# A decoder's delta-rule stage: one convolution step, one gate and two weight splits stand earlier in the engines' orders

## The reference

```python
mixed_qkv = einsum('bsh,ch->bcs', hidden, Wqkv)          # q, k: 16 heads of 128; v: 32 heads of 128
z = einsum('bsh,vh->bsv', hidden, Wz)
b, a = hidden @ Wb.T, hidden @ Wa.T
mixed_qkv = silu(causal_depthwise_conv(mixed_qkv, conv_w))   # four taps along the tokens
beta = sigmoid(b);  g = -exp(A_log) * softplus(a + dt_bias)
# per head, token by token, q and k made unit vectors first, two value heads to a key head:
state = state * exp(g_t)
delta = (v_t - state^T k_t) * b_t
state = state + k_t (x) delta;  out_t = state^T q_t
core_n = out * rsqrt(mean(out^2) + eps) * norm_w * silu(z)
result = einsum('bsv,hv->bsh', core_n, Wout)
x = layernorm(x + result)
```

## Time and profile before

| | us |
|---|---|
| median of 3 executions (3673.87 to 3677.07) | 3675.44 |
| the profiled execution's own time | 3675.6 |
| its span | 3673.6 |
| busy in the span: PE, PEld | 3177.1, 2215.0 |
| busy in the span: DVE, ACT, POOL | 2612.0, 2096.6, 1442.7 |

### The profile page before, as it was taken

The page is one execution under the profiler, slowest core; times in us unless marked ns, Lnnn a source line. Parts: engine busy times, 40 slices in busy tenths (PEclk is TensorE's granted clock), DMA queues, the critical chain, the costliest instruction groups (busy, mean ns, idle before and its releaser), DMA issues. The chain is left out here.

```text
span 3673.6 us, 81792 instructions
## 1 busy us (share of the span) xinstructions
PE 3177.1 (86%) x29389; PEld 2215.0 (60%) x29408; DVE 2612.0 (71%) x4893; ACT 2096.6 (57%) x5396; POOL 1442.7 (39%) x1753
## 2 busy tenths in 40 slices
PE   7999688437999999999999999999999999984185
PEld 5777455225676666666666667666666666762042
DVE  2333499883777777777777777677777777776896
ACT  3333300134767776677766777677776777763453
POOL 1111154103545555455544545445454454530000
PEclk9999899767999999999999999999999999996598
DMA  2000111001010010110101000111001010101201
GB/s 109 12 13 7 77 39 36 26 20 44 13 42 31 25 31 20 42 30 25 31 23 38 30 25 31 26 36 31 24 31 34 28 35 20 31 19 46 92 1 46
DMA packets 43227, 120.67 MB, mean 33 GB/s; under 512 B 5824, under 2 KB 10048, under 8 KB 39488
## 3 DMA queue, kind: packets, MB, share of 16 engines
q1 hardware_dynamic: 42816, 115.30, 9.8%
HBM read 110.75 MB, written 4.54 MB: 31 GB/s over the span
## 5 line engine op out<-in xcount | busy, mean ns | idle before, releaser
L1856 DVE TENSOR_TENSOR delta_Pb<-delta_bank,delta_lev 128x512 f16<-128x512 f32 x448 | 311.1, 694 | 240.0 <-PE delta_bank L2182 240.0
L1848 DVE SCALAR_TENSOR_TENSOR delta_F<-delta_bank,delta_cw,delta_F 128x510 f32<-128x510 f32 (+1 forms) x512 | 381.1, 744 | 66.0 <-ACT delta_far L1667 56.0
L1434 POOL TENSOR_SCALAR_AFFINE_SELECT delta_LA<-delta_LA 128x512 f32<-128x512 f32 x128 | 81.2, 635 | 858.5 <-DVE delta_LA L1877 849.2
L2156 PE MATMUL delta_bank<-delta_xh,delta_qkvh 128*128 128x512 f16 x1024 | 392.3, 383 | 4.5 <-DVE delta_qkvl L1816 3.0
L2156 PE MATMUL delta_bank<-delta_xl,delta_qkvh 128*128 128x512 f16 x1024 | 391.8, 383 | 0.0
L2156 PE MATMUL delta_bank<-delta_xh,delta_qkvl 128*128 128x512 f16 x1024 | 390.7, 382 | 0.0
L1454 POOL TENSOR_TENSOR delta_F<-delta_F,delta_far 128x506 f32<-128x506 f32 x256 | 283.2, 1106 | 256.1 <-DVE delta_F L1848 256.1
L1865 DVE CAST delta_XT<-delta_bank 128x512 f16<-128x512 f32 x448 | 309.7, 691 | 45.4 <-PE delta_bank L2205 45.2
L1661 ACT ACTIVATE delta_F<-delta_bank,delta_cw 128x512 f32<-128x512 f32 x256 | 178.2, 696 | 279.9 <-PE delta_bank L2156 279.7
L1626 ACT ACTIVATE delta_Xi<-delta_bank 128x512 f16<-128x512 f32 x320 | 189.9, 593 | 186.7 <-PE delta_bank L2201 186.7
L2141 PE MATMUL delta_bank<-delta_zh,delta_xh 128*128 128x256 f16 x1024 | 279.7, 273 | 0.6 <-ACT delta_gz L1689 0.6
(11 more groups left out here) (313 smaller groups left out, 9268.5 us busy)
## 6 DMA issues: line engine op xcount, KB each, us to landing
delta_Gb<-g_rows SPq DMA_DIRECT2D x66, 512.0 KB, 5.3
delta_st_qkv<-in_Wqkv SPq DMA_DIRECT2D x17, 1024.0 KB, 8.1
conv_T<-filters SPq DMA_DIRECT2D x32, 256.0 KB, 3.1
delta_st_zo<-in_Wz SPq DMA_DIRECT2D x16, 512.0 KB, 8.4
delta_st_zo<-in_Wout SPq DMA_DIRECT2D x16, 512.0 KB, 6.2
ffn_ahead_W<-in_W SPq DMA_DIRECT2D x2, 4096.0 KB, 17.4
conv_ahead_C<-in_ctx_rev SPq DMA_DIRECT2D x1, 6144.0 KB, 17.7
attn_xt<-in_xT SPq DMA_DIRECT2D x8, 512.0 KB, 3.8
```

The costliest lines, as they stand in the source:

```text
L1848: ve.scalar_tensor_tensor(dst, src, cw_tap(i, 3 - lag), dst, ALU.mult, ALU.add)\
L1856: ve.tensor_tensor(left(Pb[:, lvl, :, :], lvl), comp(bank[5], lvl), bc(lev[:, lvl, :].rearrange("p (n s) -> p n s", s=1 << lvl), 1, 8), AL ...
L2156: ins = te.matmul(bk[:, :], ww[:, QKV[job], kc, :], xx[:, kc, tok:tok + 512], start=(m == 0), stop=(m == 11))
```

## The change

On ACT, the two `next_o` move from behind `gate(0)` to two earlier places: the first ahead of `silu_job("q")`, the second ahead of `output_high(0)`. `gate(1)` moves from behind `level_x(2, 1)` to ahead of `silu_job("v1")`. On DVE, `next_o(0)` moves to ahead of the lags of `v0`, `next_o(1)` to where `next_o(0)` stood, and the second lag of `v1` to ahead of `level_p(2, 1)`. The instructions themselves, their sizes and their waits stay as they are, and nothing moves on PE, POOL or SP.

```diff
@@ ACT, turn @@
                 token_major(0)
+                next_o(0)
                 silu_job("q")
                 conv_tap("v0")
                 token_major(1)
                 first_answer(0)
                 silu_job("k")
+                next_o(1)
                 output_high(0)
                 output_high(1)
                 silu_job("v0")
                 gate(0)
-                next_o(0)
-                next_o(1)
                 conv_tap("v1")
                 level_x(1, 1)
                 next_qkv(0)
                 next_qkv(1)
                 first_answer(1)
+                gate(1)
                 silu_job("v1")
                 next_qkv(2)
                 level_x(2, 1)
-                gate(1)
@@ DVE, turn @@
                 level_p(0, 1)
+                next_o(0)
                 conv_lag("v0", 1, 2)
...
                 query_norm()
-                next_o(0)
+                next_o(1)
                 second_chunk()
-                conv_lag("v1", 1)
+                conv_lag("v1", 1, 2)
                 level_p(2, 1)
-                conv_lag("v1", 2)
-                next_o(1)
                 level_xt(1, 1)
```

## The result

| | before | changed |
|---|---|---|
| median, us | 3674.99 (6 runs, 3671.79 to 3677.07) | 3647.34 (6 runs, 3646.79 to 3650.75) |
| ratio | | 0.9927, 95% interval 0.9914 to 0.9939 |
| span of the profiled execution | 3673.6 | 3645.0 |

The changed kernel is 27.65 us faster; 28.4 was forecast. That the sum is this close is partly luck, as the experiments show: one term was too small, another, taken as nothing, had a cost, and the units in which the loop branches back gained more than was reckoned.

A forecast was written before the change was run, and what follows sets the result against it. PE was taken to set the pace, busy 86% of the span. Gate 17.8 plus splits 10.6, with swap and moved splits' cost 0, made 28.4 us off 3675.4: 3647.0 us, range 3638 to 3661.

The forecast's parts named there:

- the argument on `w2`: Units with splits: `w2` already waits 0.74 us for DVE's addition, so moving the second gate adds nothing there.
- The gate: Second gate ahead of `v1`'s silu on ACT: `w1`'s wait goes, 0.37 us in each of 48 units, 17.8 us.
- DVE's own row of instructions becomes the limit after 0.37: Behind `w1`, level 3's mask waited 0.37 us for L2182; with PE 0.41 earlier, DVE limits the gain to 0.37.
- The swap: Second lag of `v1` ahead of level 2's mask on DVE, 48 units without splits: gain 0, at most 0.45 us each.
- It does not shorten them: Lag and mask ahead of the copy into `XT` on DVE are only permuted, so the copy's end stays.
- So the copy still ends at 2002.87: DVE's copy into `XT` keeps its end, so L2201 still starts at 2003.02 and PE waits there instead of at `w0`.
- Which PE doesn't wait for: The earlier second lag releases POOL's far tap and ACT's silu of `v1` 0.6 us earlier, without use to PE.
- The splits: Output weight's second low half leaves DVE's row before the copy into `XT`: 0.66 us in 16 units, 10.6 us.
- A: `w0`'s wait really goes, L2201 not being held by the copy: 22 us more, 3625; chance 0.06.
- B: First split not covered ahead of `v0`'s lags, PE waits at `v1` or the answers; only the gate left: 3658; chance 0.09.
- C: Gate's gain comes back at `w2`, level 3's mask held by DVE alone; only the splits count: 3665; chance 0.05.
- D: Slower: level 2's mask waits 0.66 us for POOL's earlier far tap in all 64 units: 3689; chance 0.04.

The follow-up runs named there:

- the early copy: The changed kernel with level 1's copy into `XT` moved on DVE from behind the mask of level 2 to ahead of `second_chunk`: 3616.03 us, ratio 0.9844.

## Why the prediction was right, point by point

- **What bounds the kernel** was right: PE's stream, with DVE's row as the limit just behind it, and the two kinds of unit apart. The gate alone left the units with splits at 38.97 us, as the argument on `w2` said.
- **The gate.** The place was right, the size a little low: 0.41 us a unit alone, where I took 0.37. The failed step is "DVE's own row of instructions becomes the limit after 0.37": I took the 0.37 us of idle time for all the room there was, but recorded durations of DVE overlap a little: the mask now starts 0.14 us behind the start of the small instruction ahead of it (1991.66, 1991.80), 0.04 before that one's recorded end, so the room was 0.41.
- **The swap.** "It does not shorten them" was right, and L2200 moved nowhere but back, as said. "So the copy still ends at 2002.87" was wrong by 0.13 us: I gave the pair of lags the spacing of lag and mask. In the timeline before, the two lags of `v0` stand as one row of 1.53 us; twice 0.74 less 0.08 of overlap would be 1.40. The row could have told me. So the wait of L2200 came to 0.5 us by the bracket (31.8 in 63 times), where I had said 0.3.
- **"Which PE doesn't wait for"**, said of the silu that comes earlier, holds only with the gate moved. With the gate in its old place PE waits for just that, and the swap alone brought the same 0.3 us a unit.
- **The splits.** 0.66 us forecast, 0.67 measured alone, with the right path but luck in the size: I had left out the cast L1945, 0.25 us shorter, and the far tap that meets the low halves of the projection weights, which took as much back. The early place of the first low half came out as reckoned, blocked by POOL and covered. `cw` ended with POOL's second step again. In the changed kernel these units gave 0.77 us: 0.66 and 0.25, less 0.12 for the pair of lags, with nothing lost at the far tap, which the swap releases earlier.
- **The sum.** 13.6 + 8.3 + 5.2 = 27.1 us by the distances, 27.65 by the medians. The forecast had 48 x 0.37 and 16 x 0.66, which is 17.8, 7.9 and 2.6 us for the same three kinds. Too much for the swap and gate together (4 us) was made up mostly by the loop's returns, of which I had said nothing; that is luck. Why a shorter unit gains more there I did not follow.
- **The rivals.** A fell with the early copy: L2200 was held by the copy. B and C did not come. D did not come at the mask, which stayed at 0.68 us, but came at the low half as soon as the swap stood alone. The change as a whole escapes it because the low half left that place.

## What to carry to other kernels

A wait that the profile charges to one producer often hides a second one that ends as late two instructions on; follow PE past the gap before pricing its removal. Price a row of instructions by start-to-start steps of the same pair, not of the same instruction: a wait on the neighbour's own completion added 0.12 us here. When a row gets shorter, look at what the other engine's instructions now meet in it: a term can come out right because two such effects cancel. Two edits can remove the same wait by different ways, so measure them together and alone, and after each one ask again what is last, since the sign of the next edit can turn.

## What the runs showed of the hardware

- Two DVE instructions of 0.74 us follow each other in 0.66 us if the second waits for nothing of the first, in 0.78 us if it waits for the first's semaphore, whether or not there is a dependency in the data.
- A DVE instruction with both tensor operands in SBUF and a POOL tensor instruction on SBUF exclude each other, and the first issued goes first. The 128x512 low half took 0.74 us when it was first, 1.27 us when POOL's far tap had started 0.36 us earlier, 1.53 us when POOL's L1459 had started 0.06 us earlier; where it was held it ended 0.54 to 0.55 us behind POOL. In the other order POOL's L1487 took 1.72 us for 1.27, and the far tap 1.44 for 1.08. Masks and copies with PSUM as their source took 0.67 to 0.76 us beside POOL instructions, so none was held. The scaling `cw`, with one tensor operand in SBUF, was held: in both kernels it ended within 0.03 us of POOL's L1505.
- At the branch back of the loop a unit took 6 to 9 us longer than its like in every kernel here, and this share changed by a microsecond or so with the edits; its cause stays open. Before the change, 4.1 us of it per return were two waits of PE ahead of L2182 which nothing in the profile ended ("issue"):

```profile
PE delta_bank L2182 <- issue: 16.4, 8, 3.0
```
